# Attention in a four-stage kernel: the value products of a group issued in one piece, and the row maxima transposed by one product of 96 columns

## The reference, cut to what matters

```
q, k = _rope(q, positions), _rope(k, positions)
scores = jnp.einsum('bhqd,bhkd->bhqk', q, k) / jnp.sqrt(jnp.float32(dk))
scores = jnp.where(causal[None, None, :, :], scores, -jnp.inf)
attn = jax.nn.softmax(scores, axis=-1)
out = jnp.einsum('bhqk,bhkd->bhqd', attn, v)
return jnp.einsum('bsd,ed->bse', out.transpose(0, 2, 1, 3).reshape(B, S, H * dk), W_o)
```

## Time and profile before

| | before |
|---|---|
| median of three runs | 1900.53 us |
| the profiled execution | 1904.92 us |
| its span | 1903.1 us |
| PE busy | 1553.2 us (82%) |
| DVE busy | 1338.6 us (70%) |
| ACT busy | 1011.8 us (53%) |
| granted TensorE clock, mean | 0.895 |

### The profile page before, as it was taken

How to read it: one execution, slowest core, us unless ns; L and a number is a source line. 1 busy time by engine, 2 the same in 40 slices (tenths; PEclk the granted TensorE clock), 3 DMA queues, 4 the chain that set the end, 5 groups by cost and what they waited for, 6 DMA issues and landing times. The chain is left out here.

```text
span 1903.1 us, 22232 instructions
## 1 busy us (share of the span) xinstructions
PE 1553.2 (82%) x7115; PEld 709.6 (37%) x7115; DVE 1338.6 (70%) x1497; ACT 1011.8 (53%) x1647; POOL 1006.9 (53%) x534
## 2 busy tenths in 40 slices
PE   6788787788878877786791876788899999899998
PEld 4222222222222222221271664544555555474443
DVE  6699999998999999999662112566667776257545
ACT  5867676766666777774230432434555555446220
POOL 1599999998999999999624243201111110025000
PEclk9889888988988889987775897869999999989999
DMA  4463433243434333434003222503332221101546
GB/s 153 102 156 101 112 101 89 79 105 84 112 101 112 100 83 86 109 90 102 28 32 106 51 71 60 152 17 86 86 86 77 74 74 37 51 1 37 123 102 142
DMA packets 101777, 164.94 MB, mean 87 GB/s; under 512 B 16678, under 2 KB 55374, under 8 KB 99990
## 3 DMA queue, kind: packets, MB, share of 16 engines
q1 hardware_dynamic: 93510, 159.07, 32.7%
q0 software_dynamic: 2688, 4.80, 0.8%
q10 hardware_dynamic: 5504, 0.09, 0.2%
HBM read 106.32 MB, written 26.04 MB: 70 GB/s over the span
## 5 line engine op out<-in xcount | busy, mean ns | idle before, releaser
L481 POOL TENSOR_TENSOR PR<-H,CS 128x1024 f32<-128x1024 f32 x256 | 598.6, 2358 | 69.7 <-DVE H L457 31.4
L457 DVE TENSOR_TENSOR_SCAN H<-DA,X 128x1024 f32<-128x1024 f32 x192 | 431.2, 2273 | 0.0
L348 PE MATMUL psY<-PR,fold 128*64 128x512 f32 x1024 | 291.5, 663 | 4.5 <-POOL PR L481 4.5
L445 DVE TENSOR_TENSOR X<-DU,psB 128x1024 f32<-128x1024 f32 x192 | 235.8, 1228 | 71.8 <-PE psB L328 45.8
L433 ACT ACTIVATE DA<-DT,negA 128x511 f32<-128x511 f32 x384 | 250.6, 710 | 1.1
L1475 ACT ACTIVATE a_PT<-a_psS 128x512 f32<-128x512 f32 x320 | 181.1, 601 | 117.0 <-PE a_psS L1379 112.9
L1522 DVE TENSOR_REDUCE a_MX<-a_psM 128x1 f32<-128x384 f32 (+3 forms) x352 | 203.6, 635 | 23.6 <-PE a_psM L1394 22.2
L492 POOL TENSOR_TENSOR XS<-DU,BS 128x1024 f32<-128x1024 f32 x64 | 150.9, 2358 | 0.0
L298 PE MATMUL pp<-work,convW 128*128 (+1 forms) x256 | 145.8, 701 | 5.3 <-ACT pre L386 5.3
L1393 PE MATMUL a_psM<-a_kst,a_qst 72*128 72x512 bf16 (+3 forms) x512 | 139.0, 317 | 13.4 <-DVE a_MX L1522 10.9
L457 DVE TENSOR_TENSOR_SCAN H<-X,XS 128x1024 f32<-128x1024 f32 x64 | 146.1, 2283 | 0.5 <-POOL XS L492 0.4
(11 more groups left out here) (295 smaller groups left out, 2634.6 us busy)
## 6 DMA issues: line engine op xcount, KB each, us to landing
CS<-c_rows SPq DMA_DIRECT2D x128, 256.0 KB, 3.9
DT<-W SPq DMA_DIRECT2D x64, 256.0 KB, 4.3
DU<-ab SPq DMA_DIRECT2D x64, 256.0 KB, 4.2
BS<-c_rows SPq DMA_DIRECT2D x64, 256.0 KB, 4.3
g_CB<-c_tok SPq DMA_DIRECT2D x32, 512.0 KB, 10.9
scratch_q<-a_partsq SPq DMA_DIRECT2D x24, 384.0 KB, 3.3
a_qst<-scratch_q SPq DMA_DIRECT2D x8, 1152.0 KB
a_kst<-scratch_k SPq DMA_DIRECT2D x24, 384.0 KB
```

The costliest lines, as they stand in the source:

```text
L348: last = nc.tensor.matmul(psY[h * HP:(h + 1) * HP, n % 2 * T:(n % 2 + 1) * T], fold[:, :], chunk(PR[n % 4], h), start=False, stop=n >= NS - 2)
L445: nc.vector.tensor_tensor(both(X[s % 2][:, :]), DU[p][:, at:at + 2, :], psB[:, :].unsqueeze(1).to_broadcast([P, 2, T]), ALU.mult).then_inc ...
L457: nc.vector.tensor_tensor_scan(H[s % 4][:, :], decay, x, 0.0, ALU.mult, ALU.add).then_inc(scan_done, 1)
L481: nc.gpsimd.tensor_tensor(both(PR[s % 4][:, :]), both(H[s % 4][:, :]), CS[q % 2][:, s // 2 % 2, :].unsqueeze(1).to_broadcast([P, 2, T]), A ...
```

## The change

The four pieces of a value group are issued one behind the other, as one element of `fill`, where the elements of `items` came between them. The four transposes of the maxima's parts (24 columns each) become one of 96 columns. Its result stands in another order (by query tile, then part, then head), so `MTS` has 96 partitions of 128 elements in place of 24 of 512, and the second DMA of `send_maxima` puts the pieces of 256 bytes in the order of the rows. What is computed is the same.

```diff
-        MTS = [sb(f"MTS{i}", [24, T], BF16) for i in range(2)]
+        MTS = [sb(f"MTS{i}", [24 * QT, P], BF16) for i in range(2)]
...
             elif name[0] == "M":
-                rows = mb[:, 0:T // 2].bitcast(BF16)
-                for j in range(QT):
-                    last = nc.tensor.transpose(rows[0:24, j * P:(j + 1) * P], NMB[:, j, :, :].rearrange("p s h -> p (s h)"), identb[:, :])
+                rows, maxima = mb[:, 0:P // 2].bitcast(BF16), NMB[:, :, :, :].rearrange("p j s h -> p (j s h)")
+                last = nc.tensor.transpose(rows[0:24 * QT, :], maxima, identb[:, :])
...
-        def pe_values(pe, t, p, g, i):
-
-            if i == 0:
-                pe.wait_ge(E_done, UNITS_T * t + 10 * g + 10)
-                if g == 0:
-                    pe.wait_ge(mb_used, 9 if isinstance(t, int) and t == 0 else v_used(t))
-                n = 4 * t + g
-                if not isinstance(n, int) or n >= 1:
-                    pe.wait_ge(O_copied, n + 1)
-            for c in range(4):
-                u, col = PLACE[(c % 2, i)]
-                last = nc.tensor.matmul(psO[32 * c:32 * c + 32, i * P:T], VA[p][:, i, 4 * g + c, :],
-                                        PT[(2 * g + c // 2) % 4][u][:, col:col + T - i * P], start=i == 0, stop=i == QT - 1)
-            if i == QT - 1:
-                last.then_inc(PV_done, 1)
+        def pe_values(pe, t, p, g):
+
+            pe.wait_ge(E_done, UNITS_T * t + 10 * g + 10)
...
+            for i in range(QT):
+                for c in range(4):
+                    u, col = PLACE[(c % 2, i)]
+                    last = nc.tensor.matmul(psO[32 * c:32 * c + 32, i * P:T], VA[p][:, i, 4 * g + c, :],
+                                            PT[(2 * g + c // 2) % 4][u][:, col:col + T - i * P], start=i == 0, stop=i == QT - 1)
+            last.then_inc(PV_done, 1)
...
-                    fill += [("V", c.t, c.p, slot // 2 - 1, i) for i in range(QT)]
+                    fill.append(("V", c.t, c.p, slot // 2 - 1))
...
-                rows = mb[:, 0:T // 2].bitcast(BF16)
+                rows = mb[:, 0:P // 2].bitcast(BF16)
...
-                v.tensor_copy(MTS[half][:, :], rows[0:24, :]).then_inc(mb_used, 1)
+                v.tensor_copy(MTS[half][:, :], rows[0:24 * QT, :]).then_inc(mb_used, 1)
...
-            rows = m_scratch[ds(48 * b + 24 * half, 24), :]
+            rows = m_scratch[ds(48 * b + 24 * half, 24), :].rearrange("r (x q) -> (r x) q", q=P)
             sp.dma_start(rows, MTS[half][:, :]).then_inc(m_stored[half], 16)
             sp.wait_ge(m_stored[half], 16 * b + 16)
-            sp.dma_start(qst[pb][MROW:MROW + 3, half * 8 * T:(half + 1) * 8 * T],
-                           rows.rearrange("(s h) t -> s (h t)", s=3)).then_inc(m_loaded[half], 16)
+            sp.dma_start(qst[pb][MROW:MROW + 3, half * 8 * T:(half + 1) * 8 * T].rearrange("s (h j q) -> s h j q", h=8, j=QT),
+                           rows.rearrange("(j s h) q -> s h j q", j=QT, s=3)).then_inc(m_loaded[half], 16)
```

More of the change, by code:

```diff
@@ L1395, in pe_maxima @@
                 last.then_inc(M_ready, 1)
-        def pe_values(pe, t, p, g, i):
-            if i == 0:
-                pe.wait_ge(E_done, UNITS_T * t + 10 * g + 10)
-                if g == 0:
-                    pe.wait_ge(mb_used, 9 if isinstance(t, int) and t == 0 else v_used(t))
-                n = 4 * t + g
-                if not isinstance(n, int) or n >= 1:
-                    pe.wait_ge(O_copied, n + 1)
-            for c in range(4):
-                u, col = PLACE[(c % 2, i)]
-                last = nc.tensor.matmul(psO[32 * c:32 * c + 32, i * P:T], VA[p][:, i, 4 * g + c, :],
-                                        PT[(2 * g + c // 2) % 4][u][:, col:col + T - i * P], start=i == 0, stop=i == QT - 1)
-            if i == QT - 1:
-                last.then_inc(PV_done, 1)
+        def pe_values(pe, t, p, g):
+            pe.wait_ge(E_done, UNITS_T * t + 10 * g + 10)
+            if g == 0:
+                pe.wait_ge(mb_used, 9 if isinstance(t, int) and t == 0 else v_used(t))
+            n = 4 * t + g
+            if not isinstance(n, int) or n >= 1:
+                pe.wait_ge(O_copied, n + 1)
+            for i in range(QT):
[4 more added lines that the diff above has]
+            last.then_inc(PV_done, 1)
         V_AT = uses(True, True)["V"]
```

## The result

The changed kernel takes 1911.54 us, the median of 12 runs, against 1902.10 us for the kernel before on the same chip. The ratio of their undisturbed runs (two of the twelve of before, of 2090.68 and 2892.06 us, are left out) is 1.0066, with a 95% interval of 1.0046 to 1.0087: 12.5 us slower. I had forecast 1903 us and no change that can be told, with 0.16 for slower.

A forecast was written before the change was run, and what follows sets the result against it. PE comes closest to the bound, but the load of the stacks holds most turns. Terms +0.4 us, with the clock +3.2, on 1904.92 gave 1908.1; the median lying 4.4 lower, 1903.7, stated as 1903; range 1891 to 1913.

The forecast's parts named there:

- The cuts: Value groups on PE: each cut between pieces costs 0.2 us; seven cuts in seven turns would be 9.8 us.
- Slot 2: Slot 2: the fourth piece behind `q` goes, -0.35 us; ahead of `q` 0.22 us is added, hidden where PE waits.
- Slot 4: Slot 4: the cut is gained, then given back to `G1`'s wait for DVE's copy of `V`; 0.
- Slot 6: Slot 6: three reductions in a row delay the `MTS` copy and `G2`; shorter copy -0.12; sum +0.3 us (0 to +0.6).
- Slots 8 and 9: Slots 8 and 9: late reductions delay `MB` 0.8 us, transpose and copy return 0.3; `G3` +0.5, idle at `MB` 1.9 us.
- The DMAs: Store and load of the maxima in 96 pieces of 256 bytes: +0.3 us each, hidden.
- The cover of 3.07 us: Time from the load's issue to the next issue, released by the score unit needing it; expected to hide the DMAs' +0.3 us each.
- The clock: Idle time at `MB` brings a clock fall in about four of seven turns, half hidden: +2.8 us (0 to +10).
- The sum: All terms on the profiled execution: +0.4 us, with the clock +3.2, giving 1908.1; 1903 for the median.
- The clock falls twice a turn: Rival: idle times at `G2` (1.3 us) and `MB` (1.9) both bring falls, 20 us less about 5 hidden: 1916; chance 0.09.
- small pieces hold the scores of slot 8: Rival: store and load take 3.3 us each, maxima land some 3 us later, 1.7 us x 7: 1915; chance 0.05.

The follow-up runs named there:

- scatter: Kernel before with only the 96-column transpose, the store scattering 96 pieces into row order and the load of 3 long rows; 1876.7 us, ratio 0.9981.
- scatter_whole2: scatter with slot 2's value group in one piece, the other groups in pieces; 1873.9 us, ratio 0.9969 to the kernel before.
- whole246: Kernel before with the value groups of slots 2, 4 and 6 in one piece, slot 8 and the transposes as before; 1878.9 us, ratio 0.9988.
- whole8_warm: whole8 with 28 unread products of 128 columns in front of the wait at `MB`; 1877.8 us, ratio 0.9986 to the kernel before.
- transpose: Kernel before with only the 96-column transpose, its copy and DMAs (load in 96 pieces), value groups still in pieces; 1883.0 us, ratio 1.0018.
- whole8: Kernel before with the value group of slot 8 alone in one piece; 1888.6 us, ratio 1.0053.
- warm: Changed kernel with 28 unread products of 128 columns in front of the wait at `MB`; 1883.3 us, ratio 1.0019 to the kernel before.
- pieces: Kernel before with all value groups in one piece; transposes, `MTS` and the DMAs of the maxima as before; 1888.6 us, ratio 1.0052.
- late_scatter: Kernel before with whole groups, in slots 4, 6 and 8 behind the maxima units, 96-column transpose and scattered store; 1875.8 us, ratio 0.9979.

## Why the prediction was wrong, point by point

- **The cuts: right.** A whole group is 2.36 us, the next product 2.29 us behind its start, and PE's busy time fell by 1.9 us a turn at full clock.
- **Slot 2: right.** From `q` to the next load of the stacks it is 34.8 to 35.0 us in scatter's turns at full clock and 34.4 to 34.6 in scatter_whole2, for a forecast of -0.35 us.
- **Slot 4: right.** `G1` waits 0.60 us for DVE's copy of `V`, and the cut brings nothing. By the rule of the Trainium skill that the forecast draws on (TensorEngine Tiling (Array Packing), Key Properties) the drain's time would have come back whole; PE got it and handed it on to waits, so the trace agrees with the rule and not with the time that it alone gives.
- **Slot 6: right.** `MTS` was copied in 0.21 us, less than the 0.29 I took, three reductions took 1.62 us, 0.54 each for the 0.46 I took, and `G2` waits 1.15 us; slots 2, 4 and 6 together cost nothing that can be told (whole246, 0.9963 to 1.0012).
- **Slots 8 and 9: right as to the wait and the price.** 1.93 us for the forecast's 1.9; `MB` stands 7.8 us behind the issue of the load for 7.1 before, +0.7 for the forecast's +0.8. Without the falls it costs nothing that can be told (whole8_warm). The cover is used up by it, though: in whole8_warm's five turns PE comes to `q` after 16.7 us and never waits for the stacks, where before it waited in four of five.
- **The DMAs: wrong.** I took +0.3 us for each and all of it hidden. PE waits at slot 8 for `m_scratch`, which the forecast itself named as a sign of being wrong. The store was 1.44 us as a rule against 1.41, but 3 to 4 us at times; the load became 2.98 us from issue to use, of which 0.5 is issue. The cover of 3.07 us was used up, 0.3 us of PE's time a turn, and at times 2.3 us with the clock's fall behind it. In transpose this is 0.18%, some 3 us, and the scattered store says that up to 0.4% was to be had. The slower store that the forecast read out of the Trainium skill (DMA: Bandwidth & Descriptors, Specifications) did not show as a rule: the one in 256-byte pieces into one run of DRAM took 1.44 us. The scattered one, in pieces of the same size, took 2.0; no run separates the size from the scatter. The load's issue, of which that rule says nothing, was slower.
- **The clock: the mechanism right, the size wrong. This is the step that failed.** "I expect such a fall in about four of the seven turns, and the spare time of the load to hide half of it: +2.8 us". One fall was to be 1.4 us of work, 0.7 of it hidden. The number of falls was near, three to five of seven turns, and the size was not. The fall of the earlier trace rows is 3.4 us at half speed and not 2.9, since the window cut off its end; those behind `MB` of whole8 are 6.7 us as a rule, 13.7 once and 3.4 once. From the issue of the load to `q` PE takes 16.7 us in whole8_warm, where no fall comes; in whole8 it takes 19.1 to 19.2 in the three turns with a usual fall and 22.3 in the one with the long fall. So a fall costs 2.4 to 2.5 us, and the long one 5.6. The load could hide little of that: before, `q` stood at 16.0 to 17.4 us in the turns at full clock, at most 1.3 us beyond what PE itself needs, and the later `MB` takes 0.7 of it. In time the price of the clock at slot 8 is 1.0053 less 0.9986, 0.67% or 12.6 us of 1879, with some 5 us of doubt either way by the two intervals; the forecast had +2.8, and +10 at most. A part of it may be the load and not the clock: in whole8's one turn without a fall the stacks landed late, `q` waited 1.19 us for them and stood at 17.96.
- **The sum.** Without the clock I had +0.4 us. The changed kernel with its clock held up gives 1.0019 (warm), some 3.6 us, which is what the transposes with their DMAs cost alone (1.0018); its interval, 0.9997 to 1.0042, is too wide to test the rest of the sum.
- **The rivals.** "The clock falls twice a turn" (1916 us) and "small pieces hold the scores of slot 8" (1915) came nearer to 1911.5 us than my 1903, and neither by its own way: the falls are fewer than one a turn, each larger than I took it, and the small pieces are worth some 3 to 7 us and not 12.
- **The number.** 1911.5 us lies inside my range of 1891 to 1913, but outside the 1896 to 1909 that I gave to this mechanism. The wider range left room for other causes, so that it holds the result is luck.

## What to carry to other kernels

An order that saves an engine its own time can lengthen one of its idle times until the matrix engine's clock falls behind it, and then the stretch behind pays. So, when work is moved, write down each longer idle time of PE before and after, and the granted clock behind it, not only the sum of its waits: here 0.7 us at `MB` brought no fall, and 1.9 us brought one in about every second turn. A length alone is no rule, as the 0.78 and the 2.31 us above show. Work that nobody reads, put in front of such a wait, is the test, and here it was a cure. And where a layout has to be changed on its way through DRAM, try it on the side of the store as well as on that of the load: here the store made the kernel faster by 0.3 to 0.4%.

## What the runs showed of the hardware

- In the changed kernel the granted clock fell (2.4 to 1.2 GHz) behind an idle time of 1.93 us, between the transposes of 0.63 us and those of 1.06 us. Not every idle time of that length brought a fall: there were 12 behind 21 in the changed kernel, pieces and whole8. The 0.7 us at `MB` brought none, 0.78 us at slot 8 of transpose brought one, and 2.31 us at `q` in late_scatter none.
- Falls differ in length: 3.4 us at half speed before, and behind `MB` of whole8 6.7 us in three turns, 13.7 us in one and 3.4 us in the last.
- 28 products of 128 columns in 1.72 us of such an idle time held the clock at 1.00 in all five turns of whole8_warm and in four of warm; the fifth, at 0.99, ends with a fall behind another wait, of 1.97 us for `m_scratch`.
- A load of 24 KB in 96 pieces takes 0.72 us to issue, one in 3 long rows 0.23 to 0.26; a store of 96 pieces takes 0.32 us into one run of DRAM and 0.60 scattered.
- The scattered store had round trips of 2.0 to 2.15 us in all turns; the store of the same 96 pieces into one run had 1.44 us and single ones of 3.2 to 4.1 us. That stays unexplained.
